# Layer 2 attention: the half-width column group goes first, the ranks go ahead of the next query's transposes, and one column group is split around them

## The reference

```python
x = x + jnp.tanh(g_xattn[1]) * _L1_xattn_ref(_layernorm(x, axis=-1), ctx_2048, ctx_2048)
x = x + jnp.tanh(g_ffn[1]) * _L1_ffn_ref(_layernorm(x, axis=-1), ...)
# inside _L1_ffn_ref: routed experts, and
shared = jax.nn.silu(hidden_states @ sw_gate) * (hidden_states @ sw_up) @ sw_down
```

## Time and profile before

| what | value |
|---|---|
| median of 3 runs | 2160.2 us (2159.09 to 2166.69) |
| profiled execution: time / span | 2164.59 us / 2162.8 us |
| PE busy, of the span | 1929.2 us (89%) |
| DVE busy | 1292.1 us (60%) |
| ACT busy | 759.2 us (35%) |
| POOL busy | 845.7 us (39%) |
| granted TensorE clock, mean | 0.959 |

### The profile page before, as it was taken

How to read it: one execution, slowest core, us unless ns; L and a number is a source line. 1 busy time by engine, 2 the same in 40 slices (tenths; PEclk the granted TensorE clock), 3 DMA queues, 4 the chain that set the end, 5 groups by cost and what they waited for, 6 DMA issues and landing times.

```text
span 2162.8 us, 35551 instructions
## 1 busy us (share of the span) xinstructions
PE 1929.2 (89%) x12003; PEld 1372.2 (63%) x12003; DVE 1292.1 (60%) x3008; ACT 759.2 (35%) x2189; POOL 845.7 (39%) x838
## 2 busy tenths in 40 slices
PE   2999999989999995689999999999999869889886
PEld 2667777657777773477777777777777744333332
DVE  6999999957444442367677677776677722222221
ACT  3333333334222221555455555555555311111110
POOL 5666666536433341413333334333333231121221
PEclk9999999999999997589999999999999979999998
DMA  8433334243333334211122222221112369999995
GB/s 258 152 100 98 98 98 107 80 127 99 103 105 103 102 105 142 67 60 69 69 78 81 81 74 84 79 76 69 69 69 72 130 251 387 406 405 399 408 403 145
DMA packets 113283, 319.54 MB, mean 148 GB/s; under 512 B 31058, under 2 KB 39250, under 8 KB 104916
## 3 DMA queue, kind: packets, MB, share of 16 engines
q1 hardware_dynamic: 86244, 264.82, 33.0%
q0 software_dynamic: 26720, 52.41, 8.5%
q10 hardware_dynamic: 144, 0.03, 0.0%
HBM read 257.07 MB, written 62.06 MB: 148 GB/s over the span
## 4 chain that ended last, share of the span: by engine, by line
PE 27%; DMA 17%; DVE 10%; issue 3%; ACT 2%; POOL 1%; SPq 0%; POOLq 0%; DVEq 0%; ACTq 0%
DMA out<-routed_ym,routed_place 15%; PE attn_ffn_ps L321 12%; PE attn_score_ps L1425 4%; PE attn_tr_ps L1438 3%; DVE attn_nmax L1739 2%; PE attn_out_ps L1452 2%; PE attn_route_ps L1470 1%; ACT attn_pr L1591 1%; PE attn_score_ps L1428 1%; DVE attn_chosen L1794 1%; PE attn_tr_ps L1395 1%; DVE second_ffn_room L1744 1%; DVE attn_hot L1789 1%; DVE attn_silu_gate L1827 1%; DMA second_ffn_xg<-xn,second_ffn_pairs 1%
## 5 line engine op out<-in xcount | busy, mean ns | idle before, releaser
L1591 ACT ACTIVATE attn_pr<-attn_score_ps,attn_nmax 128x128 f32<-128x128 f32 x496 | 201.9, 419 | 184.5 <-DVE attn_nmax L1739 184.5
L1702 POOL DMA_INDIRECT list<-attn_pair,attn_pos x192 | 191.3, 996 | 65.3 <-issue 61.1
L321 PE MATMUL attn_ffn_ps<-attn_xnT_high,second_ffn_wgu_high 128*128 128x256 f32 x704 | 205.9, 292 | 5.7 <-DVE attn_hT_low L1831 4.4
L321 PE MATMUL attn_ffn_ps<-attn_xnT_low,second_ffn_wgu_high 128*128 128x256 f32 x704 | 197.2, 280 | 0.0
L321 PE MATMUL attn_ffn_ps<-attn_xnT_high,second_ffn_wgu_low 128*128 128x256 f32 x704 | 197.2, 280 | 0.0
L293 POOL TENSOR_SCALAR attn_norm_var_eps<-attn_norm_mean_var 128x2 f32<-128x2 f32 x32 | 7.4, 231 | 465.6 <-DVE attn_norm_mean_var L287 465.5
L1739 DVE TENSOR_REDUCE attn_nmax<-attn_score_ps 128x2 f32<-128x256 f32 x248 | 126.4, 551 | 66.7 <-PE attn_score_ps L1428 65.5
L1983 POOL DMA_INDIRECT out<-routed_ym,routed_place x32 | 50.2, 1569 | 294.6 <-DMA out<-routed_ym,routed_place 254.8
L1025 POOL DMA_INDIRECT y<-routed_ys,first_ffn_pair x71 | 72.3, 1018 | 181.2 <-DVE routed_ys L1181 171.3
L321 PEld LDWEIGHTS attn_ffn_ps<-attn_xnT_high,second_ffn_wgu_high 128*128 128x128 f32 x704 | 133.0, 189 | 15.9 <-DVE attn_hT_low L1831 9.5
L1438 PE MATMUL attn_tr_ps<-ident,attn_pr 128*128 128x128 f32 x768 | 114.6, 287 | 20.9 <-ACT attn_pr L1591 20.7
(11 more groups left out here) (287 smaller groups left out, 4806.4 us busy)
## 6 DMA issues: line engine op xcount, KB each, us to landing
second_ffn_room<-in_w_gu SPq DMA_DIRECT2D x16, 2816.0 KB, 30.9
second_ffn_more<-in_w_gu SPq DMA_DIRECT2D x16, 2816.0 KB, 31.4
second_ffn_room<-in_w_down SPq DMA_DIRECT2D x16, 1536.0 KB, 24.7
second_ffn_more<-in_w_down SPq DMA_DIRECT2D x16, 1536.0 KB, 24.3
wkv_x<-in_x SPq DMA_DIRECT2D x32, 512.0 KB, 4.2
second_ffn_room<-y SPq DMA_DIRECT2D x32, 512.0 KB, 5.6
wkv_vT<-in_ctxT SPq DMA_DIRECT2D x16, 512.0 KB, 4.9
xn<-wkv_xn SPq DMA_DIRECT2D x16, 512.0 KB
```

The source lines that it names most:

```text
L321: ins = nc.tensor.matmul(out, a[i], b[j], start=start and n == 0, stop=stop and n == 2)
L1591: nc.scalar.activation(pr[u % 2][:, a, j:2 * j + 1, :].rearrange("p k t -> p (k t)"), score_ps[:, a, KEYS[j]], ACT.Exp, bias=nmax[u % 2][: ...
L1702: nc.gpsimd.indirect_dma_start(io["list1"], bass.IndirectOffsetOnAxis(ap=pos[b.s][:, j, k:k + 1], axis=0), pair[b.s][:, j, k, :], None, bo ...
```

## The change

`GROUP` is a new order of the six column groups: the half-width one (number 5) first, then 0 to 4. `gate_up`, `tanh_gate` and `hidden` take their group from it, so unit 1 now has the half-width group and unit 6 a full one. `ranks` leaves the end of unit 4; in unit 5 it stands ahead of `pre`, followed by the gate columns of that unit's group (`part` 0) with the group's wait for `freed`; the up columns (`part` 1) follow `pre`, in the place where the whole group stood. The tail after the last turn keeps its order, but takes the groups in the new order too. `down` is unchanged.

```diff
+    GROUP = [M1 - 1, *range(M1 - 1)]
...
-        def gate_up(b, n):
-            pe.wait_ge(freed, FB1 * b.i + TJ + n + 1)
-
-            for col, at0 in ((0, n * P), (T, WHOLE + n * P)) if n < M1 - 1 else ((0, 2 * WHOLE),):
+        def gate_up(b, n, part=None):
+            if part != 1:
+                pe.wait_ge(freed, FB1 * b.i + TJ + n + 1)
+            g = GROUP[n]
+            parts = ((0, g * P), (T, WHOLE + g * P)) if g < M1 - 1 else ((0, 2 * WHOLE),)
+
+            for col, at0 in parts if part is None else parts[part:part + 1]:
                 for k in range(KC):
                     ins = product(nc, ffn_ps[n % 2][:, col:col + T], [w[:, k, at0:at0 + P] for w in wgu],
                                   [x[:, k, :] for x in xnT], k == 0, k == KC - 1)
-            ins.then_inc(gu_s, 1)
+            if part != 0:
+                ins.then_inc(gu_s, 1)
...
             if 0 < u <= M1:
-                gate_up(b, u - 1)
-            if u == 4:
-                ranks(b)
+                gate_up(b, u - 1, 1 if u == PRE_AT else None)
...
                 if u and u % 2 == 0:
                     back(b, u // 2 - 1)
+                if u == PRE_AT and not b.first:
+                    ranks(b.before())
+                    gate_up(b.before(), u - 1, 0)
                 if u == PRE_AT and not b.last:
                     pre(b.after())
...
         def tanh_gate(b, n):
             act.wait_ge(gu_s, M1 * b.i + n + 1)
-            nc.scalar.activation(tg[n % 2][0:width(n)], ffn_ps[n % 2][0:width(n), 0:T], ACT.Tanh, scale=0.5).then_inc(tg_s, 1)
+            r = width(GROUP[n])
+            nc.scalar.activation(tg[n % 2][0:r], ffn_ps[n % 2][0:r, 0:T], ACT.Tanh, scale=0.5).then_inc(tg_s, 1)
...
-            s, r = n % 2, width(n)
-            up = ffn_ps[s][0:P, T:2 * T] if n < M1 - 1 else ffn_ps[s][r:2 * r, 0:T]
+            s, g, r = n % 2, GROUP[n], width(GROUP[n])
+            up = ffn_ps[s][0:P, T:2 * T] if g < M1 - 1 else ffn_ps[s][r:2 * r, 0:T]
...
-            posts.need(posts.did(v.tensor_copy(hT[0][0:r, n, :], sg[s][0:r])))
-            v.tensor_tensor(hT[1][0:r, n, :], sg[s][0:r], hT[0][0:r, n, :], ALU.subtract).then_inc(freed, 1)
+            posts.need(posts.did(v.tensor_copy(hT[0][0:r, g, :], sg[s][0:r])))
+            v.tensor_tensor(hT[1][0:r, g, :], sg[s][0:r], hT[0][0:r, g, :], ALU.subtract).then_inc(freed, 1)
```

## The result

The changed kernel took 2132.5 us, the median of four runs (2131.3 to 2133.9), against 2160.3 us of the kernel before beside it (2159.1 to 2166.7). The ratio is 0.9864, with an interval of 0.9846 to 0.9882. The forecast was 2131.0 in a range of 2117 to 2144. The profiled execution of after had 2133.0 us and a span of 2131.3 us.

A forecast was written before the change was run, and what follows sets the result against it. TensorE's order of work sets a turn's length, with VectorE a second bound from unit 3 to 6. Turns 1 to 14 at 1.97 us plus 1.41 for turn 15 make 29.0, tail 0: 2160.2 - 29.0 = 2131 us, range 2117 to 2144.

The forecast's parts named there:

- VectorE's stretch: Units 3 to 6: VectorE's 18.6 us of unbroken work, beginning when TensorE delivers scores, claimed to be a second bound.
- Half group in unit 1: Unit 1: 12 fewer matmuls start VectorE's stretch 1.41 us earlier each turn; bounds 0 and 1.41.
- The rival that the head of VectorE's stretch does not move: Start of VectorE's stretch stays put, so only 0.56 us a turn is won: 2152 us, chance 0.06.
- Ranks out of unit 4: End of unit 4: unit 5's transposes start 0.87 us earlier, with 0.15 of the 0.86 us wait left.
- Gate columns ahead of pre: Unit 5: gate columns start at 1061.7 and cover pre's 0.51 us wait; unit 6's transposes start at 1066.5 instead of 1067.43.
- the second term: Unit 7's maxima on VectorE start 0.56 us earlier, giving 0.56 us a turn.
- VectorE as the next bound: Before unit 7's maxima: TensorE wins 0.9 us, but VectorE is free late, so only 0.56 us comes through.
- The remaining 0.2 us wait of unit 7: Ahead of unit 7's transposes: the full group in unit 6 leaves 0.2 of the 1.24 us wait.
- The sum: A turn gains 1.41 + 0.56 = 1.97 us, bounds 0.56 and 2.61; turn 15 gains only 1.41.
- The clock rivals: TensorE's clock falls once a turn (2155 us, chance 0.05) or twice a turn (2179 us, chance 0.04).
- The tail: After the last turn: down and the weights of pairs 2 and 3 come 1.41 us later; taken as 0, ends -9.9 and +1.4.
- the larger gain: Routed phase: gathered rows arrive without weights ahead of them because the issue order turns round; 2121 us, chance 0.13.

The follow-up runs named there:

- run 1: Kernel before with only the order of the groups changed, half-width group first; ranks and unit 5's group stay in place: 2140.0 us, ratio 0.9904.
- Runs 3 and 4: Kernel before with half-width group first, plus either ranks moved but unit 5's group unsplit (2138.8 us), or that group split but ranks left in unit 4 (2134.3 us).
- run 2: Kernel before with ranks moved and unit 5's group split, but the half-width group still last: 2159.6 us, ratio 0.9991.
- run 7: Changed kernel with the next query's norm statistics on VectorE in unit 2 instead of unit 3, except in turn 0: 2123.1 us, ratio 0.9822.
- run 9: Changed kernel plus one extra 128x384 VectorE instruction into a spare tile in unit 1 of turns 2 to 15: 2130.0 us.
- run 8: Changed kernel plus one extra 128x384 VectorE instruction into a spare tile in unit 4 of turns 1 to 15: 2140.2 us.

## Why the prediction was right

The steps, one by one. To set a time of the prediction beside after, 48.85 us are added (the turns start at 1034.86 and 1083.71) and the 1.41 subtracted that the prediction left to the end.

| step | predicted | in after | measured |
|---|---|---|---|
| transposes of unit 2 | 1041.55 | 1090.40 | 1090.40 |
| maxima at the head of VectorE's stretch | 1048.97 | 1097.82 | 1097.82 |
| transposes of unit 5 | 1059.41 | 1106.85 | 1106.85 |
| `ranks` | 1061.44 | 1108.88 | 1108.73 |
| gate columns | 1061.7 | 1109.14 | 1109.15 |
| `pre` | 1063.3 | 1110.74 | 1110.68 |
| transposes of unit 6 | 1066.5 | 1113.94 | 1113.85 |
| maxima of unit 7 | 1068.96 | 1116.40 | 1116.33 |
| full group | 1068.5 | 1115.94 | 1116.00 |
| transposes of unit 7 | 1071.79 | 1119.23 | 1119.15 |

(In the first two rows the 1.41 is already in the prediction's time.)

- **Half group in unit 1.** Right, 1.41 of 1.41, alone (run 1) and in the whole. The rival that the head of VectorE's stretch does not move fell with it.
- **Ranks out of unit 4.** The times of the steps came as written. The sum gave this part no term, but the prediction has it win 0.87 us on TensorE that the later steps build on. Runs 3 and 4 show that it has no share: 50.97 against 50.93 without the split, 50.30 against 50.29 with it. The 0.86 us that TensorE waited were slack before VectorE's copy.
- **Gate columns ahead of pre.** This is the part that makes the second term. In runs 1 and 3 the way from VectorE's copy through `pre`, the group, the values, transposes and scores back to VectorE's maxima of unit 7 ends 0.56 us late. The split takes the 12 gate matmuls, 1.41 us, out of that way, and 0.56 us of it is all that VectorE can use.
- **VectorE as the next bound.** Right: 0.56 forecast, 50.93 - 50.30 = 0.63 measured. The difference is VectorE's own stretch, from maxima to maxima 18.58 us without its wait before and 1116.33 - 1097.82 = 18.51 after: the prediction lets the maxima begin at the end of the copy's row, 0.55 us long, and in after they begin 0.47 us after its start.
- **The remaining 0.2 us wait of unit 7.** It is there, though no list names it. TensorE's last matmul of the group and ScalarE's first exponentials of unit 7 in after:

```profile
1118.82 0.28 PE L321 MATMUL attn_ffn_ps<-attn_xnT_high,second_ffn_wgu_low 128*128 128x256 f32 x1
```

```profile
1117.38 0.37 ACT L1597 ACTIVATE attn_pr<-attn_score_ps,attn_nmax 128x128 f32<-128x128 f32 x1 [2.14 <-DVE attn_nmax L1746]
```

  The transposes at 1119.15 start 0.33 us after that matmul, where 0.11 was enough in run 1, and 1.77 us after the exponentials began, which is the 1.77 of the prediction. The matmul's modelled 0.28 us hides the other 0.2.
- **The sum.** 1.97 a turn forecast, 2.04 measured. The fourteen turns gave 29.4 against 27.6: 14 x 0.07 = 1.0, and 1.55 because the fall of the clock in the turn of the earlier trace rows (53.89 us long against 52.34; its end is the first stretch of the earlier trace rows) does not come back, less 0.4 in turn 1 and 0.3 of scatter. The last turn gave 2.46 against 1.41: up to the transposes of unit 7 it gained 1.40; the other 1.06 comes after them, where the clock of before had fallen. The values of that unit, before and after:

```profile
1702.43 0.64 PE L1452 MATMUL attn_out_ps<-second_ffn_room 128*32 128x256 f32 x2 [0.62 <-DVE attn_prT L1744]
```

```profile
1673.70 0.41 PE L1453 MATMUL attn_out_ps<-second_ffn_room 128*32 128x256 f32 x2 [0.61 <-DVE attn_prT L1751]
```

  Before, these matmuls followed the 1.48 us wait of the earlier trace rows and ran at the lower clock (0.72 granted over 1700 to 1706); after, without that wait, at 1.00. In run 2 the last turn has a wait of 1.46 us in that place and no fall, and gained 1.06 us, so how often this part is won is open. The prediction counted falls of the clock as a loss that the change may bring; the falls that it takes away stand in no term of it.
- **The total.** The forecast of 2131.0 is 1.5 us from the measured median, closer than its terms are to theirs. In the profiled pair the turns gave 2.9 us more than forecast and the tail 1.7 more, while the turns began 2.1 us late; and that pair is 31.6 us apart (2164.6 to 2133.0) where the medians are 27.8 apart, since the profiled execution of before was 4.4 us above its median. That these cancel is luck.
- **The clock rivals.** They did not come: turns 2 to 15 of after were granted 1.00, and turn 1, which follows a stretch at 0.56, 0.91 (0.92 before). But run 2 shows that the mechanism is real; its place is behind the wait that ends unit 6, not unit 1 or 5 as the rivals had it. A fall costs 1.5 us, against the 1.6 estimated, and the change without its order has it in five turns of the first fourteen.
- **The tail.** The term was taken as 0, and 1.7 us came; its steps were wrong. The weights of pair 3 did not come 1.41 us later but earlier: 38.8 us after the tail's start instead of 40.6. The queue SP and then GpSimd's first two gathers, and TensorE at the first expert pair, answering; the last fence is the first gather of before, the one ahead of that in the earlier trace rows:

```profile
1724.08 0.47 SPq L2260 DMA_DIRECT2D second_ffn_more<-in_w_gu  x1
...
1725.34 1.00 POOL L2266 DMA_INDIRECT second_ffn_xg<-xn,second_ffn_pairs  x1 [8.43 <-DMA second_ffn_pairs<-list]
1726.64 0.96 POOL L2266 DMA_INDIRECT second_ffn_xg<-xn,second_ffn_pairs  x1 [0.31 <-issue]
```

```profile
1735.33 1.09 PE L2020 MATMUL routed_xt_ps<-ident,second_ffn_xg 128*128 128x128 f32 x4 [12.54 <-DMA second_ffn_xg<-xn,second_ffn_pairs]
```

```profile
1755.40 1.00 POOL L2259 DMA_INDIRECT second_ffn_xg<-xn,second_ffn_pairs  x1 [8.64 <-DMA second_ffn_pairs<-list]
```

  Before, the tail's `down` ran at the lower clock (its first matmul took 0.80 us at 1743.74 after a wait of 2.44) and after at the higher (0.50 at 1713.57 after 2.23), which outweighs the 12 matmuls. The weights of pair 3 were behind the first gather and ahead of the second before, and are ahead of both now, the opposite of the turn that the larger gain needed. The gathers still take 13.2 us to land (median), and TensorE still waits 12.5 us for the rows: the larger gain did not come. From the first gather's row to the transposes that need it there are 9.99 us now against 12.16 (1755.40 to 1767.56), so the earlier weights did not lengthen it; what shortened it is not shown. In the nine experiments the tail took 446.0 to 449.9 us, with the order of before 447.0 (run 2) and 447.7; a difference of 1.7 us in one execution of each can't be told from that scatter.

What stays open is why some waits of 1.2 to 1.5 us are followed by a fall of the clock and others of the same length are not.

## What to carry to other kernels

Before the waits of the busiest engine are added up, look for a second engine that works without a gap across them: a wait inside its stretch is worth only what it brings forward at the end of the stretch. Here the 0.86 us ahead of `ranks` were worth nothing, and the split won about what VectorE had to wait at the end, 0.6 us for its 0.56. The Trainium skill (Perfetto Trace Analysis, "Optimization Strategies") says to optimize the engines that block the critical path while TensorE waits for them. Runs 3 and 4 agree, and show that a listed wait of TensorE need not be on that path. Moving work out of the second engine's unbroken stretch into a place where it waits anyway gave 0.6 us a turn more (run 7), with nothing in the list of TensorE's waits to point to it but 0.16 us in three turns.

## What the runs showed of the hardware that I had not expected

In run 9 the extra VectorE instruction, 0.55 to 0.60 us long in run 8, took 2.6 to 3.4 us in 11 of its 14 turns. VectorE and GpSimd, one turn of the eleven and one of the other three:

```profile
1081.64 3.44 DVE L1795 TENSOR_TENSOR attn_again<-expert_no,attn_self 128x384 f32<-128x384 f32 x1
...
1232.55 0.55 DVE L1795 TENSOR_TENSOR attn_again<-expert_no,attn_self 128x384 f32<-128x384 f32 x1
```

```profile
1082.26 2.40 POOL L1694 TENSOR_TENSOR second_ffn_room<-second_ffn_room 128x1024 f32<-128x1024 f32 x1
...
1233.96 2.39 POOL L1694 TENSOR_TENSOR second_ffn_room<-second_ffn_room 128x1024 f32<-128x1024 f32 x1
```

In all eleven it ends 0.42 to 0.44 us after a GpSimd addition that began within 0.7 us of it (1085.08 against 1084.66 here); in the three turns of 0.55 us the addition begins after it has ended, or there is none. The Trainium skill (SBUF — State Buffer, "Summary: rules for kernel authors") says that a VectorE instruction with two SBUF inputs and a GpSimd instruction that reads SBUF exclude each other, the second to issue standing still until the first is done. The ends agree with that; which was issued first these rows do not show, since in some turns VectorE's row begins earlier. The same instruction, moved by three units, cost the turn 0.46 us in one place and nothing in the other, though it was up to six times as long there.
